# A two-row LSTM scan: all four gates by stationary weight tiles, the 2 columns of h streamed, x sums in PSUM banks of their own

## The chip, the cores and the metric

One core of a Trainium2 chip. TensorE (PE, with its weight loads as PEld), VectorE (DVE), ScalarE (ACT), GpSimd (POOL) and SyncE (SP) run in parallel and wait for each other through semaphores. The metric is the device time of one execution in microseconds (us); lower is better.

## The reference

Everything is fp32. `x` is (2, 1024, 256): B = 2 rows, 1024 steps. First an LSTM scan with h0 = `cond`, c0 = 0, then a modulated linear layer:

```
a = x_t @ Wx + b + h @ Wh              # (2, 1024): i, f, o, g of 256 each
c = sigmoid(f) * c + sigmoid(i) * tanh(g)
h = sigmoid(o) * tanh(c)               # hs[t] = h
x = x + hs
ys = cond / 16;  d = rsqrt((ys*ys) @ (w*w) + 1e-8)
out = x + ((x * ys) @ w) * d
```

The 1024 steps depend on each other through h and c; nearly all the time is there.

## The kernel before

Features lie on partitions, so h is 2 halves (index `j` when written, `k` when contracted, K = 2) of 128 partitions x 2 columns. A loop of NBODY = 256 bodies does T = 4 steps each (lines 265 to 306 on PE). The slot of h in `hst` for step position `s` is `t = (s + 1) % T`. x enters by groups of 4 steps (ROWS = 8 columns, packed by POOL into `xp`).

Every matmul covers 32 gate features (`c` = 0..3 selects which 32 of a half, and with that which 32 columns of the array and which 32 PSUM partitions it uses). In fp32 one matmul is two passes; each pass is one LDWEIGHTS and one MATMUL in the trace, so "x8" in a row is 4 matmuls.

- Gates i and g are *turned* (`turned`, `turned_one`, lines 218 to 230): h is the stationary operand (2, 4, 6 or 8 columns) and 64 or 32 columns of `Wh` are streamed, 20 matmuls a step. The sums lie in `pA` by rows and DVE turns them with a 32x32 transpose (line 368) into `pB`. Bias and x of these gates are put into `pA` beforehand by `fill_bias` and `fill_x` (64 columns streamed, 8 + 16 matmuls in a body).
- Gates f and o are *still* (`still`, line 232): a 128x32 tile of `Wh` is stationary and the 2 columns of h are streamed, 32 matmuls a step. Their x sums (`sum_x`, line 211, 8 columns, 32 matmuls a body) are built in `pX`, and DVE copies them with the bias into the accumulators (`carry_x`, line 352).

One step: PE waits for `h_ready[0]`, does the matmuls with k = 0, waits for `h_ready[1]`, does those with k = 1; `sums_ready[j]` releases DVE's transpose, `turned_and_fsum_ready[j]` counts the transpose and the f sums and releases ACT's sigmoid over i, f, g (line 185; g is doubled, so tanh g = 2 sigmoid(2g) - 1); DVE's two `tensor_tensor_reduce` (line 372) make c/2; ACT makes sigmoid(o) (line 190, after `osum_ready[j]`) and tanh c (192), DVE h (384). Behind the step's matmuls PE does x work: half of `sum_x` at s = 0 and at s = 1, the fills at s = 2, one filler matmul of 128 columns (line 239) at s = 3. POOL adds h to the residual (143) and packs the next x (128).

Order on each engine is the order of the code.

Of the kernel before, what the change touches and what calls it, by code (L numbers as in the profile page):

```python
# [4 lines left out]
P = 128  # L5
# [6 lines left out]
def build(nc, xT_in, condT_in, Wx, Wh, bT, bC, w, outT):  # L12
# [5 lines left out]
    PAIR = 2  # L18
    TURNED = (I_, G_)
    STILL = (F_, O_)  # L20
    T = 4
    ROWS = T * B
    NBODY = SEQ // T
# [3 lines left out]
    AT_X = 256  # L27
# [4 lines left out]
    with ctx:  # L32
# [3 lines left out]
        def sem(name):  # L36
# [64 lines left out]
        def h_slot(t):  # L101
            return (ROWS + B) * t
# [19 lines left out]
        def _(pool):  # L122
            pool.memset(bias_sb[:, :], 0.0).then_inc(bias_zeroed, 1)
            pool.memset(xh[:, :, :, 0:1], 0.0).then_inc(x_edged, 1)
            pool.memset(xh[:, :, :, 1 + SEQ:SEQ + 2 * T], 0.0).then_inc(xh_ready, T)
# [7 lines left out]
            pool.wait_ge(filled, 1)  # L133
            spread(slice(T, 2 * T))

            def bodies(lo, hi, aside=None):
                with pool.Fori(lo, hi) as it:
                    for s in range(T):
                        for j in range(K):
                            pool.wait_ge(h_ready[j], it * T + (s + 2))  # L140
                        at = h_slot((s + 2) % T)
                        now = xh[:, :, :, bass.ds(it * T + (s + 1), 1)]
                        pool.tensor_tensor(now, now, hst[:, :, at:at + B].unsqueeze(3), ALU.add).then_inc(xh_ready, 1)  # L143
                    pool.wait_ge(filled, it + 2)
                    spread(bass.ds(it * T + 2 * T, T))
                    if aside is not None:
                        aside()
# [20 lines left out]
        def _(act):  # L168
            act.dma_start(wh_sb[:, :, :], Wh.rearrange("(k p) g -> p k g", p=P)).then_inc(wh_loaded, 16)
            act.dma_start(condT[:, :, :], condT_in.rearrange("p (k b) -> p k b", k=K)).then_inc(cond_loaded, 16)  # L170
            act.wait_ge(bias_zeroed, 1)
            for n, g in enumerate(TURNED):
                act.dma_start(bias_sb[0:1, n * D:(n + 1) * D], bT[:, g * D:(g + 1) * D]).then_inc(bias_loaded, 16)  # L173
            act.dma_start(bias_col[:, :], bC[:, F_ * K:(O_ + 1) * K]).then_inc(bias_loaded, 16)
# [4 lines left out]
            with act.Fori(0, NBODY) as it:  # L179
                for s in range(T):  # L180
                    t = (s + 1) % T
                    cols = slice(B * t, B * (t + 1))
                    for j in range(K):
                        act.wait_ge(turned_and_fsum_ready[j], it * (2 * T) + 2 * (s + 1))
                        act.activation(gates[:, j, :, 0:2 * PAIR].rearrange("p b (q a) -> p a q b", a=PAIR),  # L185
                                       pB[:, j, :, 0:PAIR * Q].rearrange("p a (q r) -> p a q r", q=PAIR)[:, :, :, cols],
                                       ACT.Sigmoid).then_inc(gates_ready[j], 1)
                    for j in range(K):
                        act.wait_ge(osum_ready[j], it * T + (s + 1))
                        act.activation(ogate[:, j, :], sums[K + j][:, cols], ACT.Sigmoid)  # L190
# [7 lines left out]
        def _(pe):  # L198
            def fill_bias(j):
                for c in range(G):  # L200
                    last = pe.matmul(pA[j][c * Q:(c + 1) * Q, 0:PAIR * Q].rearrange("p (g u) -> p g u", u=Q), picks[:, :],  # L201
                                     two(bias_sb[:, :], c, j, 1), start=True, stop=False, skip_group_check=True)
                return last

            def fill_x(j, k):
                for c in range(G):
                    last = pe.matmul(pA[j][c * Q:c * Q + ROWS, 0:PAIR * Q].rearrange("p (g u) -> p g u", u=Q), xp[:, k, :],  # L207
                                     two(wx_sb[:, k, :], c, j, G_), start=False, stop=False, skip_group_check=True)
                return last

            def sum_x(n, k):
                for c in range(G):
                    last = pe.matmul(pX[c * Q:(c + 1) * Q, n * ROWS:(n + 1) * ROWS], tile(wx_sb[:, k, :], c, n % K, STILL[n // K]),  # L213
                                     xp[:, k, :], start=(k == 0), stop=(k == K - 1), skip_group_check=True)
                return last

            XSUMS = [(n, k) for n in range(PAIR * K) for k in range(K)]
            def turned(t, j, k):
                lo, M = ROWS * t, B * (t + 1)
                for c in range(G):  # L220
                    last = pe.matmul(pA[j][c * Q:c * Q + M, 0:PAIR * Q].rearrange("p (g u) -> p g u", u=Q), hst[:, k, lo:lo + M],  # L221
                                     two(wh_sb[:, k, :], c, j, G_), start=False, stop=True, skip_group_check=True)
                return last

            def turned_one(t, j, k, n):
                lo, M = ROWS * t, B * (t + 1)
                for c in range(G):
                    last = pe.matmul(pA[j][c * Q:c * Q + M, n * Q:(n + 1) * Q], hst[:, k, lo:lo + M],  # L228
                                     tile(wh_sb[:, k, :], c, j, TURNED[n]), start=False, stop=True, skip_group_check=True)
                return last  # L230

            def still(t, g, j, k, cs=range(G)):
                n = STILL.index(g) * K + j
                for c in cs:
                    last = pe.matmul(sums[n][c * Q:(c + 1) * Q, B * t:B * (t + 1)], tile(wh_sb[:, k, :], c, j, g),  # L235
                                     hst[:, k, h_slot(t):h_slot(t) + B], start=False, stop=True, skip_group_check=True)
                return last

            def filler(start):
                pe.matmul(pA[0][0:Q, P:2 * P], picks[:, :], zeros[:, :], start=start, stop=True, skip_group_check=True)  # L240
# [3 lines left out]
            for n in range(PAIR * K):  # L244
                for c in range(G):
                    pe.matmul(sums[n][c * Q:(c + 1) * Q, 0:PAIR * Q], picks[:, :], zeros[:, 0:PAIR * Q], start=True, stop=True)
            for _ in range(WARM):
                filler(True)

            pe.wait_ge(operands_ready, 3)  # L250
            for j in range(K):
                fill_bias(j)
            pe.wait_ge(xp_ready, 1)
            for n, k in XSUMS:
                last = sum_x(n, k)
            last.then_inc(x_summed, 1)
            for j in range(K):
                for k in range(K):
                    last = fill_x(j, k)
            last.then_inc(filled, 1)  # L260
            pe.wait_ge(operands_ready, 4)
            for n in range(PAIR):
                pe.wait_ge(x_carried[n], 1)
# [166 lines left out]
```

## Time and profile before

| | us |
|---|---|
| median of 3 runs | 1943.04 (1942.17 to 1943.12) |
| profiled execution | 1940.92 |
| its span | 1939.1 |
| PE, PEld busy in the span | 1739.9 (90%), 1577.4 (81%) |
| DVE, ACT, POOL busy | 1263.6 (65%), 886.4 (46%), 258.1 (13%) |
| chain that ended last | PE 72%, ACT 15%, DVE 7%, issue 5% |

Matmuls overlap: one pass lasts some 170 to 220 ns from start to modelled end, while the next starts 7 to 14 ns after it, so busy time and durations say little of PE; the differences of start times do. A run of n passes in one timeline row lasts from the first start to the last end; taking off one pass's duration gives the last start. A releaser is named in square brackets behind a row.

### The profile page before, as it was taken

To read this page: it belongs to the slowest core of one execution; us is meant where nothing else is said; L and a number is where in the kernel's file an instruction comes from. 1 tells how busy PE (TensorE), PEld (TensorE's weight loads), DVE (VectorE), ACT (ScalarE), POOL (GpSimd) and SP (SyncE) were. 2 spreads that over 40 slices of the span, in tenths; PEclk is the share of its full clock that TensorE was granted. 3 is DMA by queue.
4 is the path that set the end of the run, shared out by engine and by line. 5 is a ranking of instruction groups with operands and counts; after the bars stand their busy time and mean duration, and the time that the engine had idled before them with its cause. 6 is when DMAs were issued, how large, how long until landed. Compare 5 with 4: busy or idle time off the path is not lost.

```text
span 1939.1 us, 303170 instructions
## 1 busy us (share of the span) xinstructions
PE 1739.9 (90%) x135928; PEld 1577.4 (81%) x135928; DVE 1263.6 (65%) x12825; ACT 886.4 (46%) x6148; POOL 258.1 (13%) x1295
## 2 busy tenths in 40 slices
PE   7989899999989898989999999889898989999998
PEld 7888888888888888888888888888888888888886
DVE  4666666666666666666666666666666666666665
ACT  2444444444444444444444444444444444444443
POOL 1111111111111111111111111111111111111110
PEclk8999999999999999999999999999999999999999
DMA  3000000000000000000000000000000000000001
GB/s 94 0 0 0 0 0 0 0 0 0 0 0 0 0 0 0 0 0 0 0 0 0 0 0 0 0 0 0 0 0 0 0 0 0 0 0 0 0 0 43
DMA packets 4444, 6.68 MB, mean 3 GB/s; under 512 B 1106, under 2 KB 2900, under 8 KB 4436
## 3 DMA queue, kind: packets, MB, share of 16 engines
q1 hardware_dynamic: 3872, 5.51, 0.9%
q10 hardware_dynamic: 564, 1.05, 0.2%
q8 instruction: 6, 0.10, 0.0%
q14 instruction: 2, 0.02, 0.0%
HBM read 4.46 MB, written 2.10 MB: 3 GB/s over the span
## 4 chain that ended last, share of the span: by engine, by line
PE 72%; ACT 15%; DVE 7%; issue 5%; DMA 0%; ACTq 0%
PE pA L221 24%; PE pS L235 15%; PE pB L235 14%; ACT tanhc L192 8%; ACT ogate L190 7%; DVE hst L384 7%; PE pA L228 6%; PE pA L207 6%; PE pA L201 6%; PE pA L322 1%; DMA bias_col<-in_bC_dram 0%; PE pB L213 0%; PE pS L313 0%; ACTq L173 0%; DVE ores L399 0%
## 5 line engine op out<-in xcount | busy, mean ns | idle before, releaser
L221 PE MATMUL pA<-wh_sb,hst 128*4 128x64 f32 (+2 forms) x24576 | 654.0, 220 | 180.0 <-DVE hst L384 177.9
L185 ACT ACTIVATE gates<-pB 128x8 f32<-128x8 f32 x2048 | 351.4, 184 | 1014.6 <-DVE pB L368 1006.1
L368 DVE STREAM_TRANSPOSE pB<-pA 128x64 f32<-128x64 f32 x2048 | 444.9, 263 | 449.4 <-PE pA L221 449.3
L221 PEld LDWEIGHTS pA<-wh_sb,hst 128*4 128x4 f32 (+2 forms) x24576 | 395.2, 87 | 295.4 <-DVE hst L384 292.8
L235 PE MATMUL pS<-hst,wh_sb 128*32 128x2 f32 x32768 | 509.7, 177 | 1.5 <-issue 1.5
L372 DVE CUSTOM_DVE_ANT_1 junk<-gates 128x4 f32<-128x4 f32 x4096 | 424.6, 160 | 113.8
L235 PE MATMUL pB<-hst,wh_sb 128*32 128x2 f32 x32768 | 465.0, 174 | 0.0
L235 PEld LDWEIGHTS pB<-hst,wh_sb 128*32 128x32 f32 x32768 | 430.6, 110 | 0.0
L143 POOL TENSOR_TENSOR xh<-xh,hst 128x4 f32 (+1 forms) x1024 | 206.9, 202 | 1652.1 <-DVE hst L384 1652.1
L235 PEld LDWEIGHTS pS<-hst,wh_sb 128*32 128x32 f32 x32768 | 423.9, 108 | 1.6 <-issue 1.6
L228 PE MATMUL pA<-wh_sb,hst 128*4 128x32 f32 (+3 forms) x16384 | 423.1, 193 | 0.0
L192 ACT ACTIVATE tanhc<-gates 128x2 f32<-128x2 f32 x2048 | 381.1, 205 | 16.0
L384 DVE TENSOR_TENSOR hst<-tanhc,ogate 128x2 f32<-128x2 f32 x2048 | 328.8, 161 | 90.2 <-ACT tanhc L192 1.7
L372 DVE DVE_READ_ACCUMULATOR2_ANT gates<- 128x1 f32 x4096 | 337.9, 83 | 0.0
L228 PEld LDWEIGHTS pA<-wh_sb,hst 128*4 128x4 f32 (+3 forms) x16384 | 336.2, 88 | 0.0
L190 ACT ACTIVATE ogate<-pS 128x2 f32<-128x2 f32 x2048 | 333.3, 163 | 1.7 <-PE pS L235 1.6
L213 PE MATMUL pB<-xp,wx_sb 128*32 128x8 f32 x16448 | 228.6, 179 | 2.0 <-issue 2.0
L213 PEld LDWEIGHTS pB<-xp,wx_sb 128*32 128x32 f32 x16448 | 189.2, 111 | 10.5 <-issue 2.1
L207 PE MATMUL pA<-wx_sb,xp 128*8 128x64 f32 x8224 | 162.8, 220 | 1.4 <-issue 1.4
L207 PEld LDWEIGHTS pA<-wx_sb,xp 128*8 128x8 f32 x8224 | 129.2, 90 | 1.7 <-issue 1.7
L201 PE MATMUL pA<-bias_sb,picks 128*32 128x64 f32 x4112 | 111.0, 226 | 9.0 <-DVE wx_sb L346 0.5
L240 PE MATMUL pA<-zeros,picks 128*32 128x128 f32 x576 | 105.3, 273 | 0.1
(41 smaller groups left out, 295.5 us busy)
## 6 DMA issues: line engine op xcount, KB each, us to landing
outT_dram<-ores SPq DMA_DIRECT2D x8, 256.0 KB, 2.5
xh<-in_xT_dram SPq DMA_DIRECT2D x6, 320.0 KB
wh_sb<-in_Wh_dram ACTq DMA_DIRECT2D x1, 1024.0 KB, 8.1
wx_sb<-in_Wx_dram SPq DMA_DIRECT2D x1, 1024.0 KB, 7.6
w_sb<-in_w_dram SPq DMA_DIRECT2D x1, 256.0 KB, 6.7
xh<-in_xT_dram SPq DMA_DIRECT2D x2, 64.0 KB, 8.2
bias_sb<-in_bT_dram ACTq DMA_DIRECT2D x2, 1.0 KB
condT<-in_condT_dram ACTq DMA_DIRECT2D x1, 2.0 KB, 7.8
```

Source lines behind the costliest of these rows:

```text
L185: act.activation(gates[:, j, :, 0:2 * PAIR].rearrange("p b (q a) -> p a q b", a=PAIR), pB[:, j, :, 0:PAIR * Q].rearrange("p a (q r) -> p a ...
L190: act.activation(ogate[:, j, :], sums[K + j][:, cols], ACT.Sigmoid)
L192: act.activation(tanhc[:, j, :], gates[:, j, :, AT_C], ACT.Tanh, scale=2.0).then_inc(tanh_ready[j], 1)
L201: last = pe.matmul(pA[j][c * Q:(c + 1) * Q, 0:PAIR * Q].rearrange("p (g u) -> p g u", u=Q), picks[:, :], two(bias_sb[:, :], c, j, 1), star ...
L207: last = pe.matmul(pA[j][c * Q:c * Q + ROWS, 0:PAIR * Q].rearrange("p (g u) -> p g u", u=Q), xp[:, k, :], two(wx_sb[:, k, :], c, j, G_), s ...
L213: last = pe.matmul(pX[c * Q:(c + 1) * Q, n * ROWS:(n + 1) * ROWS], tile(wx_sb[:, k, :], c, n % K, STILL[n // K]), xp[:, k, :], start=(k == ...
L221: last = pe.matmul(pA[j][c * Q:c * Q + M, 0:PAIR * Q].rearrange("p (g u) -> p g u", u=Q), hst[:, k, lo:lo + M], two(wh_sb[:, k, :], c, j, ...
L228: last = pe.matmul(pA[j][c * Q:c * Q + M, n * Q:(n + 1) * Q], hst[:, k, lo:lo + M], tile(wh_sb[:, k, :], c, j, TURNED[n]), start=False, st ...
L235: last = pe.matmul(sums[n][c * Q:(c + 1) * Q, B * t:B * (t + 1)], tile(wh_sb[:, k, :], c, j, g), hst[:, k, h_slot(t):h_slot(t) + B], start ...
L368: dve.transpose(pT[j][:, 0:PAIR * Q], pA[j][:, 0:PAIR * Q]).then_inc(turned_and_fsum_ready[j], 1)
L372: cell = dve.tensor_tensor_reduce(out=junk[:, j, b, :], in0=gates[:, j, b, AT_I:AT_F + 1].unsqueeze(2).broadcast_to([P, 2, 2]), in1=gates[ ...
L384: dve.tensor_tensor(hst[:, j, at:at + B], tanhc[:, j, :], ogate[:, j, :], ALU.mult).then_inc(h_ready[j], 1)
```

## The change

All four gates become *still*: `TURNED`, `two`, `fill_bias`, `fill_x`, `turned`, the transposes, `bias_sb` and its two DMAs go. `pG[j]` holds the sums of i, f, g of half j, `pS[j]` those of o, `pX` the x sums of the next group in three banks of its own, `pF` the filler's output. x sums run one group further ahead: two groups are summed and one is carried in before the loop, and the slot becomes `t = (s + LEAD) % T` with LEAD = 3, so that a group begins at s = 1. The sigmoid waits for PE's `sums_ready[j]` alone.

```diff
-    TURNED = (I_, G_)
-    STILL = (F_, O_)
+    CELL_GATES = (I_, F_, G_)
+    LEAD = T - 1
+    FILL = (1, 1, 2, 1)
...
+            for n in range(1, 3):
+                pool.wait_ge(x_summed, n)
+                spread(slice(n * T, (n + 1) * T))
...
-                        act.wait_ge(turned_and_fsum_ready[j], it * (2 * T) + 2 * (s + 1))
+                        act.wait_ge(sums_ready[j], it * T + (s + 1))
...
+                        act.activation(gates[:, j, :, 0:NG].rearrange("p b n -> p n b"), cells[j][:, :, cols],
                                        ACT.Sigmoid).then_inc(gates_ready[j], 1)
...
+            def sum_x(to, j, g, k):
                 for c in range(G):
...
+                    last = pe.matmul(to[c * Q:(c + 1) * Q, :], tile(wx_sb[:, k, :], c, j, g), xp[:, k, :],
+                                     start=(k == 0), stop=(k == K - 1), skip_group_check=True)
...
+            def add_h(to, t, j, g, k, cs=range(G)):
+                for c in cs:
+                    last = pe.matmul(to[c * Q:(c + 1) * Q, B * t:B * (t + 1)], tile(wh_sb[:, k, :], c, j, g),
+                                     hst[:, k, B * t:B * (t + 1)], start=False, stop=True, skip_group_check=True)
...
                     pe.wait_ge(h_ready[0], it * T + (s + 1))
-                    turned(t, 0, 0)
-                    turned_one(t, 1, 0, 0)
-
-                    pe.wait_ge(h_ready[1], it * T + (s + 1))
-                    turned(t, 0, 1).then_inc(sums_ready[0], 1)
-                    turned_one(t, 1, 0, 1)
-                    turned(t, 1, 1).then_inc(sums_ready[1], 1)
+                    for n in range(NG):
+                        cell(t, 0, n, 0)
                     if t == 0:
                         pe.wait_ge(x_carried[1], it + 2)
+                    cell(t, 1, 0, 0)
+                    cell(t, 1, 1, 0, early)
+
+                    pe.wait_ge(h_ready[1], it * T + (s + 1))
+                    for n in range(NG):
+                        last = cell(t, 0, n, 1)
+                    last.then_inc(sums_ready[0], 1)
+                    cell(t, 1, 1, 0, late)
+                    cell(t, 1, 2, 0)
+                    for n in range(NG):
+                        last = cell(t, 1, n, 1)
+                    last.then_inc(sums_ready[1], 1)
+                    if t == 0:
+                        pe.wait_ge(x_carried[K], it + 2)
                     for j in range(K):
-                        still(t, O_, j, 0)
-                        still(t, O_, j, 1).then_inc(osum_ready[j], 1)
...
+                        add_h(outs[j], t, j, O_, 0)
+                        add_h(outs[j], t, j, O_, 1).then_inc(osum_ready[j], 1)
+
+                    if s == 0:
+                        pe.wait_ge(xp_ready, it + 3)
+                        pe.wait_ge(x_carried[0], it + 2)
+                        sum_x_cells(0)
+                    elif s == 1:
+                        pe.wait_ge(xh_ready, it * T + T)
+                        sum_x_cells(1)
+                    elif s == 2:
+                        sum_x_outs().then_inc(x_summed, 1)
                     else:
                         pe.wait_ge(xh_ready, it * T + (2 * T - 1))
-                        pe.wait_ge(gates_ready[0], it * T + (s + 1))
-                        filler(False)
+                    filler(FILL[s])
...
                         cell.then_inc(cell_ready[j], 1)
-                    if t == T - 1:
-                        dve.wait_ge(x_summed, it + 2)
-                        carry_x(0)
-                    at = h_slot((t + 1) % T)
+                        if t == T - 1 and j == 0:
+                            carry_cells(0)
                     for j in range(K):
                         dve.wait_ge(tanh_ready[j], it * T + (s + 1))
+                        at = h_slot((t + 1) % T)
                         dve.tensor_tensor(hst[:, j, at:at + B], tanhc[:, j, :], ogate[:, j, :], ALU.mult).then_inc(h_ready[j], 1)
+                        if t == T - 1 and j == 0:
+                            carry_cells(1)
                     if t == T - 1:
-                        carry_x(1)
+                        carry_outs()
```

`cell(t, j, n, k)` is `add_h` into gate n of `pG[j]`; `sum_x_cells(j)` is 24 matmuls, `sum_x_outs` 16.

PE, the first step of the loop (s = 0). Before:

```order
L221 MATMUL pA0<-wh_sb,hst 4x64 [waits h_ready0]
L221 MATMUL pA0<-wh_sb,hst 4x64 x3
L228 MATMUL pA1<-wh_sb,hst 4x32 x4
L221 MATMUL pA0<-wh_sb,hst 4x64 [waits h_ready1]
L221 MATMUL pA0<-wh_sb,hst 4x64 x3
L228 MATMUL pA1<-wh_sb,hst 4x32 x4
L221 MATMUL pA1<-wh_sb,hst 4x64 x4
L235 MATMUL pB<-hst,wh_sb 32x2 x16
L235 MATMUL pS<-hst,wh_sb 32x2 x16
L289 REGISTER_ALU
L213 MATMUL pB<-xp,wx_sb 32x8 [waits gates_ready0,xp_ready]
L213 MATMUL pB<-xp,wx_sb 32x8 x15
```

Behind 20 wide matmuls and 32 narrow ones the x work has 16, and waits for ACT and POOL.

The same step on PE now (`pG` is i, f and g, `pS` is o, `pX` the x sums, `pF` the filler):

```order
L213 MATMUL pG<-hst,wh_sb 32x2 [waits h_ready0]
L213 MATMUL pG<-hst,wh_sb 32x2 x17
L213 MATMUL pG<-hst,wh_sb 32x2 [waits h_ready1]
L213 MATMUL pG<-hst,wh_sb 32x2 x29
L213 MATMUL pS<-hst,wh_sb 32x2 x16
L275 REGISTER_ALU
L276 REGISTER_ALU [waits xp_ready]
L195 MATMUL pX<-xp,wx_sb 32x8 [waits x_carried0]
L195 MATMUL pX<-xp,wx_sb 32x8 x23
L226 MATMUL pF<-zeros,picks 32x128
```

52 matmuls of the step became 64; the x work behind them grew from 16 to 24 matmuls and now waits for DVE's `x_carried0`.

DVE, the same step before (transposes, the two halves' cells, the two halves of h):

```order
L368 STREAM_TRANSPOSE pB<-pA 128x64 [waits sums_ready0]
L368 STREAM_TRANSPOSE pB<-pA 128x64 [waits sums_ready1]
L372 ISA junk,gates<-gates 128x4 [waits gates_ready0]
L372 ISA gates 128x1
L372 ISA junk,gates<-gates 128x4
L372 ISA gates 128x1
L372 ISA junk,gates<-gates 128x4 [waits gates_ready1]
L372 ISA gates 128x1
L372 ISA junk,gates<-gates 128x4
L372 ISA gates 128x1
L384 TENSOR_TENSOR hst<-tanhc,ogate 128x2 [waits tanh_ready0]
L384 TENSOR_TENSOR hst<-tanhc,ogate 128x2 [waits tanh_ready1]
```

No carry stands in this step; the two carries were in the step at s = 2.

DVE, the same step now (line 333 carries into `pG`; the carry into `pS` follows behind these rows):

```order
L352 ISA junk,gates<-gates 128x4 [waits gates_ready0]
L352 ISA gates 128x1
L352 ISA junk,gates<-gates 128x4
L352 ISA gates 128x1
L333 TENSOR_TENSOR pG<-pX,bias_col 128x24
L352 ISA junk,gates<-gates 128x4 [waits gates_ready1]
L352 ISA gates 128x1
L352 ISA junk,gates<-gates 128x4
L352 ISA gates 128x1
L363 TENSOR_TENSOR hst<-tanhc,ogate 128x2 [waits tanh_ready0]
L333 TENSOR_TENSOR pG<-pX,bias_col 128x24
L363 TENSOR_TENSOR hst<-tanhc,ogate 128x2 [waits tanh_ready1]
```

The carry that PE's x work waits for stands behind the first half's cell; the second stands between the two halves of h.

## Rows read from the trace of the kernel before

**Rows 1.** The page, part 1: busy us, share of the span, instructions of each engine

```profile
PE 1739.9 (90%) x135928; PEld 1577.4 (81%) x135928; DVE 1263.6 (65%) x12825; ACT 886.4 (46%) x6148; POOL 258.1 (13%) x1295
```

**Rows 2.** Timeline (start us, us, engine, line), first passes of five consecutive steps

```profile
1000.93 0.29 PE L221 MATMUL pA<-wh_sb,hst 128*4 128x64 f32 x8 [0.25 <-DVE hst L384]
...
1002.75 0.30 PE L221 MATMUL pA<-wh_sb,hst 128*6 128x64 f32 x8 [0.18 <-DVE hst L384]
...
1004.57 0.30 PE L221 MATMUL pA<-wh_sb,hst 128*8 128x64 f32 x8 [0.27 <-DVE hst L384]
...
1006.52 0.29 PE L221 MATMUL pA<-wh_sb,hst 128*2 128x64 f32 x8
...
1008.34 0.30 PE L221 MATMUL pA<-wh_sb,hst 128*4 128x64 f32 x8 [0.25 <-DVE hst L384]
```

**Rows 3.** Timeline, one step at s = 0 (1001 to 1002.6 us)

```profile
1001.04 0.24 PE L228 MATMUL pA<-wh_sb,hst 128*4 128x32 f32 x8
...
1001.10 0.30 PE L221 MATMUL pA<-wh_sb,hst 128*4 128x64 f32 x8
...
1001.38 0.44 PE L235 MATMUL pB<-hst,wh_sb 128*32 128x2 f32 x31
1001.46 0.43 DVE L368 STREAM_TRANSPOSE pB<-pA 128x64 f32<-128x64 f32 x2 [0.42 <-PE pA L221]
...
1001.65 0.19 PE L235 MATMUL pS<-hst,wh_sb 128*32 128x2 f32 x1
1001.66 0.17 PE L235 MATMUL pB<-hst,wh_sb 128*32 128x2 f32 x1
1001.67 0.48 PE L235 MATMUL pS<-hst,wh_sb 128*32 128x2 f32 x31
1001.79 0.34 ACT L185 ACTIVATE gates<-pB 128x8 f32<-128x8 f32 x2 [0.94 <-DVE pB L368]
1002.00 0.16 DVE L372 CUSTOM_DVE_ANT_1 junk<-gates 128x4 f32<-128x4 f32 x1
...
1002.11 0.17 ACT L190 ACTIVATE ogate<-pS 128x2 f32<-128x2 f32 x1
1002.12 0.44 PE L213 MATMUL pB<-xp,wx_sb 128*32 128x8 f32 x32
...
1002.18 0.16 DVE L372 CUSTOM_DVE_ANT_1 junk<-gates 128x4 f32<-128x4 f32 x1
...
1002.30 0.20 ACT L192 ACTIVATE tanhc<-gates 128x2 f32<-128x2 f32 x1
...
1002.41 0.15 ACT L190 ACTIVATE ogate<-pS 128x2 f32<-128x2 f32 x1
1002.46 0.20 ACT L192 ACTIVATE tanhc<-gates 128x2 f32<-128x2 f32 x1
1002.53 0.33 DVE L384 TENSOR_TENSOR hst<-tanhc,ogate 128x2 f32<-128x2 f32 x2
```

**Rows 4.** Groups by line and shape: busy us, mean ns of one | idle before

```profile
L240 PE MATMUL pA<-zeros,picks 128*32 128x128 f32 x576 | 105.3, 273 | 0.1
...
L355 DVE TENSOR_TENSOR pB<-pB,bias_col 128x16 f32<-128x16 f32 x257 | 45.6, 178 | 0.8 <-PE pB L213 0.8
```

**Rows 5.** Timeline of PE, the filler at s = 3

```profile
1000.30 0.38 PE L240 MATMUL pA<-zeros,picks 128*32 128x128 f32 x2
```

**Rows 6.** Timeline, PE before the loop and in its first body

```profile
11.06 0.69 PE L213 MATMUL pB<-xp,wx_sb 128*32 128x8 f32 x62
...
16.22 0.23 PE L221 MATMUL pA<-wh_sb,hst 128*6 128x64 f32 x2 [1.67 <-issue]
...
27.85 0.28 PE L235 MATMUL pS<-hst,wh_sb 128*32 128x2 f32 x5 [1.51 <-issue]
```

**Rows 7.** Stretch 12 to 31 us: busy by engine, PEclk, DMA share, GB/s

```profile
12.00:31.00 19.00, 12.07 (x696) 10.76 (x687) 6.58 (x64) 4.37 (x30) 1.19 (x6) 0.65 0.02 4
```

**Rows 8.** DMA queues: packets, MB, share of 16 engines

```profile
q8 instruction: 6, 0.10, 0.0%
```

More of the change, by code:

```diff
@@ L101, in h_slot @@
         def h_slot(t):
[L102 removed]
+            return B * t
         @block.sync
@@ L140, in bodies @@
                             pool.wait_ge(h_ready[j], it * T + (s + 2))
[L141 to L145, printed above, removed]
+                        if s == T - 1:
+                            pool.wait_ge(x_summed, it + 3)
+                            spread(bass.ds(it * T + 3 * T, T))
+                        now = xh[:, :, :, bass.ds(it * T + (LEAD + s), 1)]
+                        pool.tensor_tensor(now, now, hst[:, :, h_slot(s):h_slot(s) + B].unsqueeze(3), ALU.add).then_inc(xh_ready, 1)
                     if aside is not None:
@@ L170, in _ @@
             act.dma_start(condT[:, :, :], condT_in.rearrange("p (k b) -> p k b", k=K)).then_inc(cond_loaded, 16)
[L171 to L174, printed above, removed]
+            act.dma_start(bias_col[:, :, :], bC[:, 0:K * NG].rearrange("p (j n) -> p j n", n=NG)).then_inc(bias_loaded, 16)
+            act.dma_start(bias_o[:, :], bC[:, K * NG:]).then_inc(bias_loaded, 16)
             act.wait_ge(zeros_ready, 1)
@@ L189, in _ @@
                         act.wait_ge(osum_ready[j], it * T + (s + 1))
-                        act.activation(ogate[:, j, :], sums[K + j][:, cols], ACT.Sigmoid)
+                        act.activation(ogate[:, j, :], outs[j][:, cols], ACT.Sigmoid)
                         act.wait_ge(cell_ready[j], it * T + (s + 1))
@@ L211, in sum_x @@
[L211 to L237, printed above, removed]
@@ L239, in filler, with sum_x_cells @@
-            def filler(start):
-                pe.matmul(pA[0][0:Q, P:2 * P], picks[:, :], zeros[:, :], start=start, stop=True, skip_group_check=True)
+                    last = pe.matmul(to[c * Q:(c + 1) * Q, :], tile(wx_sb[:, k, :], c, j, g), xp[:, k, :],
+                                     start=(k == 0), stop=(k == K - 1), skip_group_check=True)
+                return last
+            def sum_x_cells(j):
+                for n, g in enumerate(CELL_GATES):
+                    for k in range(K):
+                        last = sum_x(xcells[j][:, n, :], j, g, k)
+                return last
@@ new lines, in sum_x_outs @@
+            def sum_x_outs():
+                for j in range(K):
+                    for k in range(K):
+                        last = sum_x(xouts[:, j, :], j, O_, k)
+                return last
+            def add_h(to, t, j, g, k, cs=range(G)):
+                for c in cs:
+                    last = pe.matmul(to[c * Q:(c + 1) * Q, B * t:B * (t + 1)], tile(wh_sb[:, k, :], c, j, g),
+                                     hst[:, k, B * t:B * (t + 1)], start=False, stop=True, skip_group_check=True)
+                return last
@@ new lines, in cell, with clear, filler @@
+            def cell(t, j, n, k, cs=range(G)):
+                return add_h(cells[j][:, n, :], t, j, CELL_GATES[n], k, cs)
+            def clear(of):
+                for c in range(G):
+                    pe.matmul(of[c * Q:(c + 1) * Q, :], picks[:, :], zeros[:, 0:of.shape[1]], start=True, stop=True)
+            def filler(count, start=False):
+                for _ in range(count):
+                    pe.matmul(pF[0:Q, 0:P], picks[:, :], zeros[:, :], start=start, stop=True, skip_group_check=True)
@@ L242, in _ @@
             pe.wait_ge(zeros_ready, 1)
             pe.wait_ge(operands_ready, 1)
[L244 to L248, printed above, removed]
-            pe.wait_ge(operands_ready, 3)
[L251 to L263, printed above, removed]
+            for j in range(K):
+                clear(pG[:, j, 0:NG * ROWS])
+                clear(outs[j])
+            filler(WARM, True)
+            pe.wait_ge(operands_ready, 2)
+            for n in range(2):
+                pe.wait_ge(xp_ready, n + 1)
+                for j in range(K):
+                    if n:
+                        pe.wait_ge(x_carried[j], n)
+                    sum_x_cells(j)
+                if n:
+                    pe.wait_ge(x_carried[K], n)
+                sum_x_outs().then_inc(x_summed, 1)
@@ L265, in _ @@
+            pe.wait_ge(operands_ready, 3)
+            early, late = range(G // 2), range(G // 2, G)
             with pe.Fori(0, NBODY) as it:
                 for s in range(T):
-                    t = (s + 1) % T
+                    t = (s + LEAD) % T
                     pe.wait_ge(h_ready[0], it * T + (s + 1))
-                    turned(t, 0, 0)
-                    turned_one(t, 1, 0, 0)
-                    pe.wait_ge(h_ready[1], it * T + (s + 1))
-                    turned(t, 0, 1).then_inc(sums_ready[0], 1)
@@ L349, in _, with carry_cells, carry_outs @@
             for j in range(K):
-                dve.tensor_copy(hst[:, j, h_slot(1):h_slot(1) + B], condT[:, j, :]).then_inc(h_ready[j], 1)
-            def carry_x(n):
-                at = n * K * ROWS
-                into = pS if n else pB[:, :, 1, :]
-                dve.tensor_tensor(into[:, :, 0:ROWS], pX[:, at:at + K * ROWS].rearrange("p (j r) -> p j r", r=ROWS),
-                                  bias_col[:, n * K:(n + 1) * K].unsqueeze(2).broadcast_to([P, K, ROWS]),
-                                  ALU.add).then_inc(x_carried[n], 1)
+                dve.tensor_copy(hst[:, j, h_slot(LEAD):h_slot(LEAD) + B], condT[:, j, :]).then_inc(h_ready[j], 1)
+            def carry_cells(j):
+                dve.tensor_tensor(cells[j][:, :, 0:ROWS], xcells[j], bias_col[:, j, :].unsqueeze(2).broadcast_to([P, NG, ROWS]),
+                                  ALU.add).then_inc(x_carried[j], 1)
+            def carry_outs():
+                dve.tensor_tensor(pS[:, :, 0:ROWS], xouts, bias_o[:, :].unsqueeze(2).broadcast_to([P, K, ROWS]),
+                                  ALU.add).then_inc(x_carried[K], 1)
+            dve.wait_ge(bias_doubled, 1)
             dve.wait_ge(x_summed, 1)
-            for n in range(PAIR):
-                carry_x(n)
+            for j in range(K):
+                carry_cells(j)
+            carry_outs()
             with dve.Fori(0, NBODY) as it:
                 for s in range(T):
-                    t = (s + 1) % T
-                    for j in range(K):
-                        dve.wait_ge(sums_ready[j], it * T + (s + 1))
-                        dve.transpose(pT[j][:, 0:PAIR * Q], pA[j][:, 0:PAIR * Q]).then_inc(turned_and_fsum_ready[j], 1)
+                    t = (s + LEAD) % T
                     for j in range(K):
@@ L416 @@
         "Wh": _np.ascontiguousarray(inputs["L0_cond_Wh"]),
-        "bT": _np.ascontiguousarray(_np.asarray(inputs["L0_cond_b"]).reshape(1, 4 * d)),
-        "bC": _np.ascontiguousarray(_np.asarray(inputs["L0_cond_b"]).reshape(4 * d // 128, 128).T),
+        "bC": _np.ascontiguousarray(_np.asarray(inputs["L0_cond_b"]).reshape(4, d // 128, 128)[[0, 1, 3, 2]].transpose(2, 1, 0).reshape(128, -1)[:, [j * 4 + n for j in range(d // 128) for n in range(3)] + [j * 4 + 3 for j in range(d // 128)]]),
         "w": _np.ascontiguousarray(inputs["L1_cond_weight"]),
```

98 lines of the change are left out of this document (33 added, 65 removed).

## Prediction

> **What bounds it now.** I read the page's busy shares first: PE and its weight loads fill most of the span, no other engine comes near [rows 1]. That does not yet say PE is the limit, so next the timeline by steps: five first passes give steps of 1.82, 1.82, 1.95 and 1.82 us, 7.41 a body [rows 2]. Only the 1.95 begins without a wait for h in its bracket: there PE itself was late (the wide fills). The other three are a ring, which the timeline of one step shows [rows 3]. Turned matmuls 1000.93 to 1001.38, f passes behind them; DVE's transposes start at 1001.46, ACT's sigmoids at 1001.79, the cell at 1002.00, tanh at 1002.30, h at 1002.53, PE again at 1002.75 [rows 2, 3]. Two things end together ahead of the sigmoid: the first transpose (1001.46 plus about 0.26) and the 16th f pass (about 1001.49, plus the 0.28 that a PE result needs, below). So dropping the transposes alone would save little; what counts is how soon the new passes are through.
>
> **Prices, all from start differences.**
> - Pass of 64 columns: 0.11/8 = 14 ns (1000.93 to 1001.04); of 32 columns 0.06/8 = 7.5 ns [rows 2, 3].
> - Pass of 2 columns: the f and o run has 64, first start 1001.38, last 1001.67 + 0.48 - 0.17 = 1001.98: 0.60/63 = 9.5 ns. Passes of 8 columns: 32 in 0.44 - 0.18, 8.4 ns [rows 3]; 62 before the loop in 0.69 - 0.18, again 8.4 ns [rows 6]. The f/o run has three passes inside that raise a semaphore (each 16th), the x runs have none. I split it so: 8.2 ns a pass and 0.028 us per raise (63 x 8.2 = 0.517, the rest 0.083 over 3). Bounds: 7.5, and 9.5 with nothing for a raise.
> - PE's last pass to the consumer: the k = 1 group of half 0 starts at 1001.10 and its eight passes within 0.07 to 0.10, the transpose at 1001.46: 0.26 to 0.29, I take 0.28. Sigmoid to cell 0.21, cell to tanh 0.30, tanh to h 0.23, h to PE 0.22, of which h itself is half of 0.33, so DVE to PE 0.06. Ogate to tanh need be only 0.05 apart (1002.41, 1002.46). First to second half's cell 0.18 [rows 3].
> - Filler: its second pass starts 0.38 - 0.27 = 0.11 after its first, so 0.22 a filler on its column group [rows 4, 5].
> - A carry: 0.18 for 16 elements [rows 4]; I take 0.18 for 24 too.
>
> The Trainium skill, "TensorE: Matmul & The Clock Gate", section "The cost: per-tile semaphore tail", puts 26.3 ns on each increment. That is close to the 0.028 of my split: by it the sum below holds, while 9.5 ns for every pass would make it 2060 us.
>
> **The change, step by step (time 0 = first pass of a step).** A step has 64 matmuls, 128 passes, instead of 104 passes, and none is wide. Raises stand after passes 60 (sums 0), 96 (sums 1), 112 and 128 (o).
> - Ring, j = 0: sums 0 at 60 x 8.2 = 0.49, sigmoid 0.77, cell 0.98, tanh could go at 1.28 (before: 1002.30 - 1000.93 = 1.37). But o of half 0 is pass 112: 0.918 + 2 x 0.028 = 0.97, ogate 1.25, tanh 1.30, h 1.53, PE 1.75. So a wait for o takes the place of the transposes, and the ring shortens from 1.82 to 1.75 only. Half 1: sums 1 at 0.82, sigmoid 1.10, cell 1.31, tanh 1.61, h 1.84, at PE 2.06 = 0.31 into the next step; the k = 0 passes ahead of that wait last 36 x 8.2 = 0.30. No loss.
> - s = 3: ring, 1.75. Its filler and the loop branch fit before it (PE done at 1.16 + 0.22).
> - s = 1: PE needs 1.05 + 0.11 for the step, 48 x passes 0.39, filler 0.22: 1.78. The filler uses one column group, the raises another, and a group can run a little ahead of the others: an o pass starts at 1001.65 before the last f pass at 1001.66 [rows 3]. So I let the ring decide: 1.75.
> - s = 2: 1.16, 32 x passes 0.26, a raise 0.03, two fillers 0.44: 1.89; counted on the filler's column group alone (40 passes x 33 ns + 0.44) 1.75. I take 1.82. PE sets this one.
> - s = 0: x work must wait until DVE has carried the old x sums of half 0 out of `pX`: cell 0 at 0.98 + 0.18, carry 0.18, 0.06 to PE: 1.40, though PE was ready at 1.16. Queued behind this wait on PE are 48 x passes 0.39, a filler 0.22, and with them the next step's first pass, for which the whole ring waits: 2.01.
> - Hidden: the other two carries (DVE is free between the halves of h, and h is not late before 2.01), POOL's pack of x, which now goes ahead of its add (POOL is busy 13% [rows 1], the pack begins with the step and is needed at 1.40; each 0.1 that it came later would cost 26 us). SP's queue is as before; ACT issues one DMA less.
>
> Body 2.01 + 1.75 + 1.82 + 1.75 = 7.33 or 7.34 against 7.41: 256 x -0.07 = -18 us; I write -17.
>
> Once: before the loop 256 x passes (2.1 us) instead of 64 narrow and 48 wide (1.2), plus a round trip to POOL and DVE for the second group: about +1.7. In the first body PE stands still four times for nothing that the profile shows a releaser for, 1.67 first and 1.51 last [rows 6], while the instruction queue's packets arrive [rows 8]: code being loaded, 1060 PE records of a body (265 matmuls, 4 each). 1300 records mean one or two gaps more: +2.5. The granted clock is 0.65 over 12 to 31 us [rows 7], part of it at the 1.2 GHz level, and a longer start lengthens that: about +2.5. Together +6.5 (1 to 12).
>
> Sum against the profiled execution: 1940.9 - 17 + 6.5 = 1930; the median shown lies 2.1 above it: 1932 us.
>
> **What the unknown price does.** Per ns of pass price a body moves by about 0.49 us (108, 112, 160 and 112 passes on the four paths), 126 us in all. At 7.5 ns the body is 7.0 and the time 1842; at 9.5 (no raises) 2.16 + 1.89 + 1.96 + 1.84 = 7.85 and 2060. The sign turns at about 8.3 ns, so this is a forecast with little behind its sign.
>
> **Rivals.**
> - PE becomes the bound (slower). 162 passes a step on average instead of 133 (135928/1024) [rows 1]; if the long unbroken run settles at 8.7 ns instead of 8.2 the body is 7.58 and the time 1940.9 + 44 + 6.5 + 2 = 1993. For it: the only 2-column run shown does 9.5. Against: its raises, and both x runs at 8.4. Decides from 8.3 ns.
> - Larger gain. Column groups run apart, so fillers and raises overlap, and a run keeps near 7.8: body 7.14, 1880 us. For it: 7.5 ns at 32 columns, the passes out of order in rows 3. Against: 8.4 in both x runs.
> - The loop's code no longer stays loaded: one gap a body, 256 x 1.6 = +410, 2340 us. Rows 8 show 6 packets in the whole run, so 256 branches back reloaded nothing with 1060 records. The Trainium skill, "Runtime: NRT & Kernel Launch", section "Instruction fetch mechanics", says that a taken branch to a page outside the current two forces a fetch; this trace disagrees for the loop before, and whether 1300 records still fit no run shows.
> - The change doesn't do what it says: the sigmoid released by the f passes as much as by the transposes, and o now later: no change, within a body of 7.37 to 7.40.
>
> **Chances.** Forecast's own case (body 7.20 to 7.37, 1896 to 1939) 0.36; larger gain 0.16; no change 0.12; PE the bound 0.33; reloads 0.03. A difference under 0.2% (3.9 us) can't be told from no change here. Faster 0.52, same 0.12, slower 0.36. Own range of the forecast 1896 to 1939; to leave out no more than 2 in 10 it must take in most of both neighbours: 1875 to 2005.
>
> **What would show it.** Steps of about 2.0, 1.75, 1.8, 1.75 in the timeline; no `DVE` transposes, ACT's sigmoid released by PE, tanh right behind ogate (0.05); PE idle 0.2 at s = 0 until a carry ends; a pass price of 8.2 ns and a jump of 0.03 behind each raise. Wrong if the o run ends later than 1.25, if the steps with x work are all near 1.9, or if PE shows gaps without a releaser in every body.

## The result, and the profile after

The changed kernel takes 2815.84 us (median of 4 runs, 2813.99 to 2817.97) against 1943.08 for the kernel before: ratio 1.4491 [1.4466, 1.4516]. The forecast was 1932 us, the range 1875 to 2005.

The page of the changed kernel: busy shares, the clock in 40 slices, the instruction queue, and the head of the chain that ended last.

```profile
PE 2797.3 (99%) x166792; PEld 2642.5 (94%) x166792; DVE 929.9 (33%) x11034; ACT 881.3 (31%) x6148; POOL 250.2 (9%) x1295
...
PEclk6555555555555555555555555555555555555556
...
q8 instruction: 8, 0.13, 0.0%
...
PE 99%; issue 0%; DVE 0%; DVEq 0%
```

PE has gone from 90% [rows 1] to 99% and is the whole chain. The PEclk row points to the reason: 5 in every slice but the ends, so half of full speed (a granted clock of 1.00 is 2.4 GHz, 0.50 is 1.2 GHz, the two levels of TensorE's clock). q8 has 8 packets against 6 [rows 8]: the longer body is not loaded again.

Stretches of the changed kernel (us, PE, PEld, DVE, ACT and POOL busy, PEclk, DMA share, GB/s):

```profile
0.00:12.00 12.00, 10.68 (x222) 9.89 (x223) 1.70 (x13) 1.49 (x2) 0.60 (x7) 1.00 0.56 188
12.00:40.00 28.00, 16.37 (x972) 15.20 (x972) 5.09 (x59) 4.35 (x30) 1.50 (x8) 0.57 0.02 4
40.00:80.00 40.00, 40.00 (x2416) 38.12 (x2415) 12.90 (x156) 12.55 (x88) 3.34 (x18) 0.50 0.19 56
80.00:2790.00 2710.00, 2710.00 (x163020) 2568.62 (x163019) 903.05 (x10787) 860.57 (x6021) 244.16 (x1260) 0.50 0.00 0
```

and of the kernel before, from 31 us on:

```profile
31.00:80.00 49.00, 44.41 (x3510) 40.57 (x3503) 31.95 (x326) 22.54 (x156) 6.56 (x33) 1.00 0.15 46
80.00:1939.00 1859.00, 1673.11 (x131563) 1516.50 (x131546) 1223.02 (x12422) 858.02 (x5960) 249.03 (x1248) 1.00 0.00 1
```

Both start at 2.4 GHz and fall to 1.2 GHz in pauses at the start, four before and seven now [rows 6, 7]. I read them as code being loaded: the profile shows no releaser for them, and the changed kernel has none from 40 us on. Before, the clock is back at 1.00 from 31 us on. After, it stays at 0.50 for 2710 us in which PE's records leave no gap.

What that costs, in PE's timeline of the changed kernel (start us, us, line):

```profile
2001.25 0.28 PE L213 MATMUL pG<-hst,wh_sb 128*32 128x2 f32 x6
...
2003.92 1.48 PE L213 MATMUL pG<-hst,wh_sb 128*32 128x2 f32 x96
2005.22 0.61 PE L213 MATMUL pS<-hst,wh_sb 128*32 128x2 f32 x32
2005.65 0.83 PE L195 MATMUL pX<-xp,wx_sb 128*32 128x8 f32 x48
2006.31 0.40 PE L226 MATMUL pF<-zeros,picks 128*32 128x128 f32 x1
...
2012.06 0.28 PE L213 MATMUL pG<-hst,wh_sb 128*32 128x2 f32 x6
```

From 2003.92 on the first 96 passes of a step take 1.30 from the first start to the first of the next 32, which is 13.5 ns each. The first and the last row are first passes of a step, one body apart: 10.81 us, times 256 = 2767, and 47 for start and end make the span of 2814.

### The profile page after: what moved, and what is told of

It reads as the page before. It is cut to its first block, busy times and chain, and to the rows that moved or that the text cites. A ratio compares the mean times of both kernels' runs of the same rounds, so it can differ in the third digit from the quotient of the medians.

```text
span 2814.0 us, 360822 instructions
## 1 busy us (share of the span) xinstructions
PE 2797.3 (99%) x166792; PEld 2642.5 (94%) x166792; DVE 929.9 (33%) x11034; ACT 881.3 (31%) x6148; POOL 250.2 (9%) x1295
## 4 chain that ended last, share of the span: by engine, by line
PE 99%; issue 0%; DVE 0%; DVEq 0%
PE pG L213 48%; PE pF L226 18%; PE pX L195 17%; PE pS L213 16%; PE pX L301 1%; PE pS L292 0%; DVE ores L380 0%; PE pG L222 0%; PE pS L222 0%; DVE pG L333 0%; DVE zeros L308 0%; DVE picks L307 0%; DVE picks L310 0%; DVEq L341 0%
## 5 line engine op out<-in xcount | busy, mean ns | idle before, releaser
L213 PEld LDWEIGHTS pG<-hst,wh_sb 128*32 128x32 f32 x98304 | 1708.4, 150 | 128.0 <-DVE hst L363 92.9
L213 PE MATMUL pG<-hst,wh_sb 128*32 128x2 f32 x98304 | 1730.4, 195 | 2.6 <-issue 2.6
L180 ACT ACTIVATE gates<-pG 128x6 f32<-128x6 f32 x2048 | 370.7, 181 | 1874.9 <-PE pG L213 1874.9
L226 PE MATMUL pF<-zeros,picks 128*32 128x128 f32 x2624 | 747.5, 411 | 0.0
L213 PE MATMUL pS<-hst,wh_sb 128*32 128x2 f32 x32768 | 682.4, 193 | 2.9 <-issue 2.9
L195 PE MATMUL pX<-xp,wx_sb 128*32 128x8 f32 x33024 | 625.2, 201 | 6.3 <-issue 5.9
L213 PEld LDWEIGHTS pS<-hst,wh_sb 128*32 128x32 f32 x32768 | 623.3, 154 | 3.0 <-issue 3.0
L195 PEld LDWEIGHTS pX<-xp,wx_sb 128*32 128x32 f32 x33024 | 563.6, 153 | 6.7 <-issue 6.2
L226 PEld LDWEIGHTS pF<-zeros,picks 128*32 128x32 f32 x2624 | 314.2, 160 | 19.3
L333 DVE TENSOR_TENSOR pG<-pX,bias_col 128x24 f32<-128x24 f32 x514 | 94.8, 185 | 3.4 <-PE pX L195 3.4
```

The lines of the kernel that those rows point to most:

```text
L180: act.activation(gates[:, j, :, 0:NG].rearrange("p b n -> p n b"), cells[j][:, :, cols], ACT.Sigmoid).then_inc(gates_ready[j], 1)
L195: last = pe.matmul(to[c * Q:(c + 1) * Q, :], tile(wx_sb[:, k, :], c, j, g), xp[:, k, :], start=(k == 0), stop=(k == K - 1), skip_group_che ...
L213: last = pe.matmul(to[c * Q:(c + 1) * Q, B * t:B * (t + 1)], tile(wh_sb[:, k, :], c, j, g), hst[:, k, B * t:B * (t + 1)], start=False, sto ...
L226: pe.matmul(pF[0:Q, 0:P], picks[:, :], zeros[:, :], start=start, stop=True, skip_group_check=True)
L333: dve.tensor_tensor(cells[j][:, :, 0:ROWS], xcells[j], bias_col[:, j, :].unsqueeze(2).broadcast_to([P, NG, ROWS]), ALU.add).then_inc(x_car ...
```

## Experiments

Theory A: the clock only lacks something that raises it after these pauses. B: the new loop cannot hold 2.4 GHz. C: the passes are slow at any clock. In this section a time is that of a single run; only those of g1, g2, h1 and h2 are medians of 4.

**e1: a burst after each 64 bodies.** The loop on PE is split in four, and behind each part stands

```diff
+    pe.matmul(pF[:, :], wx_sb[:, 0, 0:P], wx_sb[:, 0, 0:512], ...)   # 24 times
```

> The 256 bodies in four quarters of 64, and after each quarter TensorE runs 24 matmuls of 128x128 by 512 columns that nobody reads. Theory A (the granted clock fell to the 1.2 GHz level in the pauses of the first body and the loop only lacks something that raises it again): quarter 1 at 0.50 and 10.9 us a body, from the first burst on 1.00 and about 7.3 us a body; time about 18 + 699 + 3 x 64 x 7.34 + bursts and end 55 = 2180 us. Theory B (the passes of 2 and 8 columns do not hold the full clock even once it is granted): each burst is at 1.00 in its second part, the clock is back at 0.50 soon behind it, 10.9 us a body in all four quarters; time about 2816 + 4 x 12 = 2860 us. Theory C (the passes themselves are slow, whatever the clock): clock 1.00 behind a burst and still 10.9 us a body.

2894.07 us. Stretches around the first burst, and PE's timeline behind the second:

```profile
700.00:715.00 15.00, 15.00 (x948) 14.40 (x944) 4.97 (x62) 4.96 (x36) 1.16 (x6) 0.50 0.00 0
715.00:730.00 15.00, 15.00 (x176) 7.86 (x170) 1.11 (x12) 1.01 (x8) 0.56 (x3) 0.75 0.00 0
730.00:740.00 10.00, 10.00 (x25) 4.46 (x24) 0.00 (x0) 0.00 (x0) 0.00 (x0) 1.00 0.00 0
740.00:750.00 10.00, 9.90 (x700) 8.34 (x701) 3.56 (x43) 3.48 (x24) 0.77 (x5) 0.82 0.00 0
750.00:770.00 20.00, 20.00 (x1233) 19.24 (x1230) 6.35 (x76) 6.16 (x43) 1.75 (x10) 0.50 0.00 0
```

```profile
1452.17 0.99 PE L213 MATMUL pG<-hst,wh_sb 128*32 128x2 f32 x94
...
1453.56 0.57 PE L195 MATMUL pX<-xp,wx_sb 128*32 128x8 f32 x47
...
1454.03 0.21 PE L213 MATMUL pG<-hst,wh_sb 128*32 128x2 f32 x3
...
1455.92 1.01 PE L213 MATMUL pG<-hst,wh_sb 128*32 128x2 f32 x94
...
1457.70 0.20 PE L213 MATMUL pG<-hst,wh_sb 128*32 128x2 f32 x2
...
1459.56 1.28 PE L213 MATMUL pG<-hst,wh_sb 128*32 128x2 f32 x94 [0.21 <-DVE hst L369]
```

The burst raises the clock, and it falls again 5 to 8 us behind each of the first three, though PE hardly pauses: it is busy for 9.90 of the 10 us from 740, and the gap ahead of 1459.56 is 0.21 us. A falls, B stands. C falls too: at 2.4 GHz one whole body takes 1459.56 - 1452.17 = 7.39 us. It is one body, begun with the other engines waiting for PE; by it the changed kernel at full clock would only have matched the 7.41 of before, and all of the loss is clock.

**e2 to e4: other fillers.** e2 sets `FILL = (0, 0, 0, 0)`; e3 and e4 put one 128x128 by 512 matmul, as in the burst, behind step 3 or behind every step.

> The changed kernel without its five fillers a body. If TensorE at the half clock is the only bound, a body loses 5 x 0.42 = 2.1 us: 8.8 us a body, 2280 us, clock 0.50 throughout. If the ring of engines bounds it in spite of TensorE's 99%, it stays near 2816 us. If the fillers are what keeps the clock from falling further or rising, the clock differs from 0.50.

> The five fillers of a body are replaced by one matmul of 128x128 by 512 columns behind step s = 3. Theory A and B both: if this raises the granted clock, the body is that of the forecast without fillers, 1.79 + 1.75 + 1.75 + 1.75 = 7.04 us, about 1860 us, clock near 1.00. If not, TensorE at half clock: 10.9 - 2.1 + 0.87 = 9.7 us a body, about 2500 us, clock 0.50. Theory C: 9 us or more a body at any clock.

> As the one before, with a matmul of 128x128 by 512 columns behind every step. If the clock rises and holds: 2.2 + 2.0 + 1.9 + 1.75 = 7.8 us a body, about 2050 us. If it stays at 0.50: 10.9 - 2.1 + 4 x 0.87 = 12.3 us a body, about 3160 us. If one wide matmul a body is too little and four are enough, this run is faster than the one before.

2412.12, 2814.71 and 4422.14 us, clock 0.50 from 40 us on in all three. e2: 404 us less, 1.58 a body, so PE was the limit, and the fillers alone neither cause nor cure the low clock. I expected 2.1: without fillers PE is busy 96%, and ACT and DVE hold 5% of the chain that ended last. In e3 and e4 I had the matmul too cheap: (4422 - 2412)/1024 = 1.96 us a step more at half clock, not 0.87.

**e5 to e8: wide dummies on all four column groups** (the four sets of 32 array columns), which nobody reads, behind each step. e5 has the old filler once for each group (the 32 ahead of the loop become 8 for each), e6 256 columns for each, and e7 and e8

```diff
+    for cols in (64, 32, 64, 32, 64):      # e8: (64, 64)
+        for c in range(G):
+            pe.matmul(pF[c*Q:c*Q+8, 0:cols], wx_sb[:, 0, 0:8], wh_sb[:, 0, c*64:c*64+cols], ...)
```

> Every filler of the changed kernel runs on all four column groups in place of one (four matmuls of 128x32 by 128 columns each, 20 a body for 5). The groups run beside each other, so at an unchanged clock the time should hardly move. Theory B1 (what raises and holds the clock is streaming on all four column groups for a good part of the time, as the wide passes of the kernel before did): clock near 1.00, body about 7.5 us, 1960 us. Theory B2 (fillers of this kind do nothing, the clock needs TensorE busy with wide passes in one unbroken stretch, as in a burst): clock 0.50, 10.9 to 11.2 us a body, 2820 to 2900 us.

> No fillers; behind each step four matmuls of 128x32 by 256 columns, one for each column group, of real numbers in place of zeros. B1: clock near 1.00, about 0.43 us more a step than without: body 7.04 + 2 x 0.43 to 4 x 0.43 = 7.9 to 8.7 us, 2040 to 2250 us. B2: clock 0.50, 9.3 + 4 x 0.98 = 13.2 us a body, 3400 us.

> No fillers; behind each step the turned passes of the kernel before are put back as dummies that nobody reads: 12 matmuls that stream 64 weight columns and 8 that stream 32, over all four column groups, with 8 stationary columns. B1: they raise and hold the clock as they did in the kernel before: clock near 1.00, body about 7.7 us, 1990 us. B2, or if what held the clock before was something else (its pauses, its fills): clock 0.50, 9.3 + 4 x 0.74 = 12.2 us a body, 3150 us.

> As the one before with 8 dummy matmuls of 64 columns a step in place of 20 of 64 and 32. If a share of the wide passes is enough: clock near 1.00, body about 7.4 us, 1920 us, which would beat both kernels. If the clock wants more of them: 0.50, 9.3 + 4 x 0.32 = 10.6 us a body, 2740 us.

2817.25, 3112.39, 3108.31 and 2685.57 us, mean clocks 0.50 to 0.51: B1 falls for raising. (e6 I had too dear: (3112 - 2412)/1024 = 0.68 us a step more, not 0.98.) Putting the old wide passes beside the new narrow ones (e7) does not bring the clock back.

**f1 to f4: the same four with one burst.** e8, e7, e5 and e6 with 10 matmuls of the burst behind the first body, and again behind the last, so that the second body starts at 2.4 GHz.

> e8 (no fillers, 8 dummy matmuls of 64 columns a step) with one burst of 10 matmuls of 128x128 by 512 columns behind the first body. Theory H: raising the clock needs more than holding it; the burst raises it, and the dummies hold what the changed kernel's own passes could not: clock about 0.99, body about 7.4 us, 18 + 11 + 15 + 255 x 7.4 + 17 = 1950 us. Theory N: these dummies do not hold it either: back to 0.50 within some 10 us of the burst, 2686 + 13 = 2700 us.

> e7 (no fillers, the 20 dummy matmuls of 64 and 32 columns a step, as many as the kernel before had) with the one burst behind the first body. H: clock 0.99, body about 7.7 us, 2020 us. N: 0.50 again, 3108 + 13 = 3120 us. If f1 falls back and this one holds, it is a matter of how much is streamed.

> e5 (fillers of 128 columns on all four column groups, 1, 1, 2 and 1 behind the steps) with the one burst. H: clock 0.99, body 7.4 to 7.5 us, 1950 to 1980 us. N: 0.50 again, 2817 + 13 = 2830 us; since with fillers on one column group the clock fell 7 to 14 us after each burst, this tells whether the other three groups count.

> e6 (no fillers, 256 columns on each of the four column groups behind each step) with the one burst. H: clock 0.99, body 7.9 to 8.7 us, 2080 to 2280 us. N: 0.50 again, 3112 + 13 = 3125 us.

2704.75, 3125.04, 2831.09 and 3116.96 us: N, none holds it. Stretches of f4, then of f2:

```profile
42.00:75.00 33.00, 32.57 (x2285) 26.01 (x2285) 11.76 (x142) 11.30 (x78) 3.10 (x16) 1.00 0.22 68
76.00:3000.00 2924.00, 2924.00 (x164182) 2488.29 (x164179) 877.41 (x10504) 834.43 (x5863) 239.25 (x1228) 0.50 0.00 0
```

```profile
53.00:1000.00 947.00, 947.00 (x63314) 936.07 (x63310) 284.67 (x3403) 270.51 (x1900) 79.47 (x402) 0.50 0.01 2
1029.00:1032.00 3.00, 2.90 (x305) 2.75 (x301) 1.08 (x13) 0.88 (x6) 0.56 (x3) 0.99 0.00 0
```

f4 held it to 75 us, some 27 us behind its burst, and in f2 it rose for a moment with no burst near and fell again.

**g1 to g3: the streaming of 2 columns alone undone.** h lies in zeroed slots of `WID` columns and every pass with h streams the whole slot: 32 columns in g1 and g2, 16 in g3; g2 keeps the fillers, g1 and g3 have none.

```diff
-    return B * t
+    return (WID + B) * t
...
-    pe.matmul(to[c*Q:(c+1)*Q, B*t:B*(t+1)], ..., hst[:, k, B*t:B*(t+1)], ...)
+    pe.matmul(to[c*Q:(c+1)*Q, :], ..., hst[:, k, WID*t:WID*(t+1)], ...)
```

> The changed kernel with one part undone: a pass with h streams 32 columns, the 2 of h and 30 zeros, in place of the 2 alone; no fillers. At the full clock a pass of 32 columns costs no more than one of 2 (7 to 8 ns against 8.2 to 8.8). Theory W (the granted clock follows how many columns the passes stream): about 2000 columns a step, as many as the wide passes of the kernel before had, so the clock rises behind the loading pauses and holds: 0.99, body 1.85 + 1.80 + 1.75 + 1.85 = 7.25 us, 18 + 15 + 256 x 7.25 + 17 = 1905 us. Theory U (whatever 128x32 weight loads for each small pass do is the cause, not the columns): clock 0.50, passes of 16 ns in place of 13.6, body 9.3 + 512 x 0.0024 = 10.5 us, 2720 us.

> As the one before, with the fillers of the changed kernel left as they are, so that the 30 columns of zeros are the only difference from it. W: clock 0.99, the body that the changed kernel showed behind a burst, 7.39 us, 1940 us. U: 0.50, 10.9 + 1.2 = 12.1 us a body, 3130 us.

> As g1 with 16 columns. W, if half the columns are enough: clock 0.99 and 1905 us; if not, 0.50 and, with passes of 14 ns, 9.3 us a body, 2420 us. U: the same 2420 us.

g1 1905.64 us, ratio to the kernel before 0.9819 [0.9803, 0.9836]; g2 1976.30, 1.0182 [1.0165, 1.0199]; g3 1882.72; mean clock 0.99 in all three. g2 differs from the changed kernel by the 30 columns of zeros alone: 1976 against 2816 us. U falls.

**g4: the other direction.** The kernel before, its turned passes cut to 8 and 4 columns; it leaves h out of most sums of gates i and g and serves for its time only.

> The other direction: the kernel before with the same instructions, but its turned passes stream only the first 4 units of 32 of each gate (8 and 4 columns in place of 64 and 32; the sums of the other units leave h out). W: with less to do it loses its clock: 0.50 for most of the loop, a step of about 2.0 us, 2100 us. U: the clock stays at 0.99 and it becomes a little faster than before, 1850 to 1940 us.

2055.76 us, mean clock 0.57:

```profile
15.00:59.00 44.00, 38.32 (x2510) 35.34 (x2510) 23.34 (x236) 16.32 (x113) 4.37 (x22) 0.50 0.17 52
59.60:62.90 3.30, 2.87 (x275) 2.62 (x262) 2.33 (x24) 1.73 (x12) 0.58 (x3) 1.00 0.00 0
63.00:1000.00 937.00, 923.05 (x63191) 853.23 (x63187) 592.05 (x5964) 411.93 (x2862) 120.95 (x602) 0.56 0.00 0
```

With as many instructions and less to stream, the kernel before loses its clock too, but for rises of a few us such as the one at 59.6, and is slower by 115 us.

**h1 and h2: how narrow.** h1 is g3 again, h2 has 8 columns (`WID = 8`), both without fillers.

> The kernel of g3 again (16 columns, no fillers), timed in rounds: if its one time was no accident, 1880 to 1886 us, 3% under the kernel before, and clock 0.99.

> As g1 with 8 columns, a quarter. By theory W there is a width from which the clock is lost, and 2 lies below it. If 8 lies above: clock 0.99, body 7.10 us, 1870 us. If below: 0.50 for all or most of the loop, between 1900 and 2420 us by the share of it that runs at the full clock. Sixteen columns gave 0.99; I expect 8 to lie below, since the x passes stream 8 columns and did not hold it in the changed kernel.

h1 1881.34 us, 0.9693 [0.9677, 0.9709]. h2 1875.79, **0.9667 [0.9651, 0.9683]**, the fastest: I expected 8 columns to lose the clock, and they hold it. The page and two stretches of h2:

```profile
PE 1675.9 (90%) x164232; PEld 1577.3 (84%) x164232; DVE 915.6 (49%) x11034; ACT 901.2 (48%) x6148; POOL 251.0 (13%) x1295
...
PEclk7999999999999999999999999999999999999999
```

```profile
12.00:41.00 29.00, 18.05 (x1325) 17.26 (x1328) 6.59 (x79) 6.08 (x42) 1.58 (x9) 0.59 0.01 4
41.00:80.00 39.00, 35.00 (x3449) 33.02 (x3444) 19.15 (x235) 19.05 (x131) 5.37 (x28) 1.00 0.19 58
```

h2 has PE less busy than the changed kernel (90% to 99%) and a higher clock. It also refutes W as I put it: a step of h2 streams 64 x 8 columns of h and, on average, 16 x 8 of x, 640 in all; one of f2 64 x 2 + 16 x 8 + 12 x 64 + 8 x 32 = 1280, and f2 fell. The sum of columns does not decide. That in this loop the width of 2 costs the clock is shown (e2 and h2 differ by the width alone: 2412 and 1876 us). Passes of 2 columns as such do not: the kernel before has them in 32 of its 52 matmuls with h in a step and holds 2.4 GHz. What the chip weighs is open.

## Why the prediction was wrong, point by point

- **The step that failed** is in "Once": "The granted clock is 0.65 over 12 to 31 us [rows 7], part of it at the 1.2 GHz level, and a longer start lengthens that: about +2.5." It took the return to 2.4 GHz for granted, whatever PE does in the loop. All prices of the sum were read at 2.4 GHz. What came in its place: 1.2 GHz to the end, (10.81 - 7.39) x 256 = 876 us. No rival had it, although the 0.65 showed that this kernel visits the low level. The change also takes away the passes that were there when it rose; in the kernel before:

```profile
31.09 0.42 PE L221 MATMUL pA<-wh_sb,hst 128*6 128x64 f32 x8
...
31.39 0.29 PE L221 MATMUL pA<-wh_sb,hst 128*6 128x64 f32 x8
```

  Eight wide passes last 0.42 us, and eight more, 0.3 us later, the 0.29 of [rows 2]: the clock rises here, with PE busy throughout since 27.85 [rows 6].
- **The ring** was right at 2.4 GHz, as far as h2 shows it with 8 columns. The forecast had sigmoid 0.77 behind a step's first pass, cell 0.98, ogate 1.25, tanh 1.30, h 1.53, PE 1.75. One step of h2:

```profile
1000.12 1.00 PE L214 MATMUL pG<-hst,wh_sb 128*32 128x8 f32 x94
...
1000.88 0.51 ACT L181 ACTIVATE gates<-pG 128x6 f32<-128x6 f32 x2 [0.80 <-PE pG L214]
...
1001.09 0.17 DVE L353 CUSTOM_DVE_ANT_1 junk<-gates 128x4 f32<-128x4 f32 x1 [0.73 <-ACT gates L181]
...
1001.36 0.17 ACT L185 ACTIVATE ogate<-pS 128x2 f32<-128x2 f32 x1
...
1001.43 0.20 ACT L187 ACTIVATE tanhc<-gates 128x2 f32<-128x2 f32 x1
...
1001.66 0.44 DVE L364 TENSOR_TENSOR hst<-tanhc,ogate 128x2 f32<-128x2 f32 x2
...
1001.88 1.00 PE L214 MATMUL pG<-hst,wh_sb 128*32 128x8 f32 x94
...
1003.64 1.00 PE L214 MATMUL pG<-hst,wh_sb 128*32 128x8 f32 x94
...
1005.40 1.00 PE L214 MATMUL pG<-hst,wh_sb 128*32 128x8 f32 x94 [0.47 <-DVE hst L364]
...
1007.25 1.00 PE L214 MATMUL pG<-hst,wh_sb 128*32 128x8 f32 x94
```

  0.76, 0.97, 1.24, 1.31, 1.54 and 1.76: the wait for o took the place of the transposes [rows 3], as forecast. The split into 8.2 ns a pass and 0.028 a raise gives 94 x 8.2 + 0.028 = 0.80 for the 0.82 that e1 and h2 took; with the same raise that is about 8.4 ns a pass, where the forecast's sign turned at 8.3. By e1's body, 7.39 for 7.41, the forecast gain of 11 us was not there at 2.4 GHz either.
- **s = 0** waits for the carry: x work at 1.39 behind the first pass in e1 (1452.17 to 1453.56), forecast 1.40. What follows was mis-sized: the filler runs beside x passes, so e1 needs 1.86 for the step, not 2.01.
- **The sum of a body**, 7.34, measured 7.39 in e1: s = 1, 2 and 3 took 1.89, 1.78 and 1.86 for 1.75, 1.82 and 1.75. The fillers, which I called hidden at s = 1 and s = 3, were not: g1 and g2 differ by them alone, (1976.30 - 1905.64)/256 = 0.28 us a body. Without them, and with 8 columns, the three steps take 1.76 each in h2, and a body 7.13 (1000.12 to 1007.25). In [rows 2] it is the pass at the end of the 1.95, at 1006.52, that has no wait, and not the one at its start; the reading that PE was late there stands.
- **Once**: h2's span less 256 x 7.13 leaves 47 us, the kernel before 1939 less 256 x 7.41 leaves 42: +5 for a forecast of +6.5. Of pauses I counted one or two more; there are three more. Reloading of the body: refuted by q8. The Trainium skill, "Runtime: NRT & Kernel Launch", section "Instruction fetch mechanics", speaks of a fetch when a branch goes outside the current two pages of 256 instructions; by that each branch back over the 1300 records would fetch, and 8 packets in the run again disagree. By the 2048 instructions for which that section of the Trainium skill gives PE room the body stays loaded, as it did.
- **PE the bound** came true for a reason that its rival did not have: not 8.7 ns a pass but 13.5, at 1.2 GHz.

## What to carry to other kernels

A price holds only at the clock at which it was read. Where a trace shows two levels, ask what PE did when the clock rose, and whether the change keeps that; a page that says 99% busy does not say full clock. Narrowing the streamed operand saved nothing here (at 2.4 GHz a step's first 94 passes take 0.82 us with 2 columns in e1 and with 8 in h2), and padding it with zeros to 8 columns turned a loss of 24% (e2) into a gain of 3.3% (h2), without fillers in both.

## What the hardware showed that I had not expected

- PE busy in its records without a gap for 2710 us, at 1.2 GHz throughout. The Trainium skill, "TensorE: Matmul & The Clock Gate", section "Part 1: The HAM clock gate", ties the low clock to idleness; by that this loop would run at 2.4 GHz, and the trace disagrees.
- Holding the clock differs by program, and not by idle time in the records: h2 with PE 90% busy holds 2.4 GHz, f1 to f4 lose it in stretches of 4 to 5 us in which PE is busy 95% or more (4.80 of 5 us in f1, 4.90 in f2, 4.76 in f3, 4.00 of 4 us in f4).
- A narrow pass takes 13.5 ns at 1.2 GHz for 8.7 at 2.4 (0.82/94, raise included), not twice as long.
